# Attention heads each in their own half of the TensorE rows, paired maxima, and a causal mask set on the exponentials

## The reference

```
c_kv   = x @ W_dkv.T
q_lat  = einsum('bhtd,hdl->bhtl', q, k_eff)
attn   = einsum('bhtl,bsl->bhts', q_lat, c_kv) / sqrt(hs)      # hs = 16
attn   = where(causal_mask, -inf, attn);  attn = softmax(attn)
y      = attn times values, head by head
x      = x + layernorm(attention(layernorm(x)))
x      = x + layernorm(experts(layernorm(x)))
```

## Time and profile before

| what | value |
|---|---|
| median of 3 runs | 1568.74 us (1567.91 to 1570.16) |
| profiled execution, first to last instruction (its span; the profile gives no other time of its own) | 1560.5 us |
| median less this span | 8.2 us |
| PE busy | 1174.1 us, 75% |
| PE weight loads busy | 873.2 us, 56% |
| DVE busy | 925.3 us, 59% |
| ACT busy | 657.4 us, 42% |
| POOL busy | 340.4 us, 22% |
| mean granted TensorE clock | 0.861 |

### The profile page before, as it was taken

The page is one execution under the profiler, slowest core; times in us unless marked ns, Lnnn a source line. Parts: engine busy times, 40 slices in busy tenths (PEclk is TensorE's granted clock), DMA queues, the critical chain, the costliest instruction groups (busy, mean ns, idle before and its releaser), DMA issues. The chain is left out here.

```text
span 1560.5 us, 26871 instructions
## 1 busy us (share of the span) xinstructions
PE 1174.1 (75%) x8433; PEld 873.2 (56%) x8434; DVE 925.3 (59%) x2241; ACT 657.4 (42%) x1097; POOL 340.4 (22%) x316
## 2 busy tenths in 40 slices
PE   6844499999999999999933506977978979899000
PEld 3423255555555555555423406977978978899000
DVE  6514466666776666767178526576575665755245
ACT  3420055545554555555735413432433424344322
POOL 4104000000000000000036764034033030300785
PEclk9975699999999999999965557999989989899555
DMA  5973222222222222220011234122121221111324
GB/s 156 292 191 113 79 73 77 79 83 72 80 83 83 70 83 81 82 72 14 2 56 54 94 121 149 47 89 85 53 87 38 93 81 57 30 47 40 93 80 157
DMA packets 82934, 133.23 MB, mean 85 GB/s; under 512 B 26549, under 2 KB 53445, under 8 KB 82789
## 3 DMA queue, kind: packets, MB, share of 16 engines
q1 hardware_dynamic: 67304, 80.83, 17.1%
q0 software_dynamic: 15552, 51.42, 10.2%
HBM read 75.82 MB, written 55.87 MB: 84 GB/s over the span
## 5 line engine op out<-in xcount | busy, mean ns | idle before, releaser
L699 DVE TENSOR_REDUCE att_pm<-att_ps_m 128x1 f32<-128x512 f32 (+3 forms) x640 | 353.2, 592 | 168.9 <-PE att_ps_m L559 98.5
L673 ACT ACTIVATE att_pt<-att_ps_s 128x1024 f32<-128x1024 f32 (+3 forms) x384 | 304.8, 811 | 272.1 <-PE att_ps_s L600 192.2
L1354 ACT ACTIVATE moe_hf<-moe_ps_h,moe_b 128x256 f32<-128x256 f32 x288 | 136.9, 475 | 296.3 <-PE moe_ps_h L1305 238.6
L556 PE MATMUL att_ps_m<-att_k,att_q 128*128 128x512 f32 (+3 forms) x576 | 213.6, 420 | 10.7 <-DMA att_v<-vs 9.2
L1380 DVE TENSOR_TENSOR moe_hTl<-moe_hf,moe_hTh 128x256 fp32r<-128x256 f32 x288 | 165.4, 574 | 9.8
L596 PE MATMUL att_ps_s<-att_q,att_k 128*128 128x512 f32 (+3 forms) x576 | 164.1, 369 | 1.6 <-ACT att_pt L673 1.6
L556 PEld LDWEIGHTS att_ps_m<-att_k,att_q 128*128 128x128 f32 x576 | 112.8, 199 | 85.0 <-issue 76.7
L1378 DVE CAST moe_hTh<-moe_hf 128x256 fp32r<-128x256 f32 x288 | 118.9, 413 | 32.7 <-ACT moe_hf L1354 32.7
L613 PE MATMUL att_ps_o<-att_pt,att_v 128*17 128x512 f32 (+3 forms) x1152 | 118.8, 491 | 0.0
L559 PE MATMUL att_ps_m<-keep_mask_ts,keep_identb 128*128 128x128 bf16 x512 | 118.5, 237 | 0.0
L596 PEld LDWEIGHTS att_ps_s<-att_q,att_k 128*128 128x128 f32 x576 | 96.2, 192 | 33.2 <-ACT att_pt L673 25.6
(11 more groups left out here) (203 smaller groups left out, 2530.3 us busy)
## 6 DMA issues: line engine op xcount, KB each, us to landing
weights_raw<-in_w POOLq DMA_DIRECT2D x14, 1024.0 KB, 7.3
ys<-att_zeros POOLq DMA_DIRECT2D x10, 1024.0 KB, 9.5
moe_rows<-xs SPq DMA_DIRECT2D x38, 256.0 KB, 2.7
ys<-moe_o SPq DMA_DIRECT2D x36, 256.0 KB, 2.2
att_q<-qs SPq DMA_DIRECT2D x48, 128.0 KB
att_k<-ks SPq DMA_DIRECT2D x48, 128.0 KB
vs<-proj_v SPq DMA_DIRECT2D x32, 136.0 KB, 7.6
proj_x<-in_x POOLq DMA_DIRECT2D x8, 512.0 KB, 6.3
```

The costliest lines, as they stand in the source:

```text
L556: ins = pe.matmul(out[:, n * keys:(n + 1) * keys], qg[slot][:, h // 2, i * P:(i + 1) * P], kg[slot][:, h, k0:k0 + keys], start=True, stop= ...
L673: act.activation(pt[:, blk % 3, 2 * p:2 * p + 2, off:CH], ps_s[k % 2][:, :, off:CH], ACT.Exp, scale=HS ** -0.5).then_inc(ex_done, 1)
L699: return dve.tensor_reduce(pm[:, g % 2, i, piece, h:h + 1], src, AX.X, ALU.max)
L1354: act.activation(hf[:, f % NHB], ps_h[f % NHB][:], ACT.Relu, bias=b1[r][:, f:f + 1]).then_inc(hf_done, 1)
```

## The change

- Keys are stored like queries: `k` has two places of 128 rows instead of four, head `h` in rows `64*(h%2)` on. Each matmul of queries and keys reads only the 50 rows of its head (`rows = slice(64*e, 64*e + KM)`), and the matmuls of the heads `e = 0` and `e = 1` are issued one behind the other into different banks. The zeros and their memsets are gone, with the waits for them.
- Units are made two at a time. A pair waits for both of its banks, and signals both at its end. There are 38 units a group instead of 44: the 128-key rest of row block 4 shares a bank with row block 0, and the 256-key rests of row block 5 are two heads to a bank. The maxima are kept in another order (`pm`), and one reduction can write two places.
- The mask of a unit's diagonal block is two accumulating matmuls of 64 columns and 64 rows, `pick` times `future`, for each head.
- The exponent pass has no mask matmul. GpSimd sets the exponentials above the diagonal to zero in place (`affine_select` on 128 x 4 x 128 values) for the 8 diagonal blocks of the 12, after the second exponential of the block; the values of these blocks wait for it (`masked`).
- The two turns of the maxima move from after steps 15 and 17 to after step 18. All jobs of a step come ahead of its value block; before, only the first did.
- The clears of `ys` (16 of 640 rows) and the loads of `keep_xf` move from GpSimd's queue to SyncE's.

```
     slots["q"].append(s.sb(f"q{g}", [P, 2, T], F32R))
-    slots["k"].append(s.sb(f"k{g}", [P, GH, T], F32R))
+    slots["k"].append(s.sb(f"k{g}", [P, 2, T], F32R))
...
+    for e in range(2):
+        add((e, e + 2), ((0, 0, P, 0), (4, CH, P, 8)))
+    for e in range(2):
+        add((e, e + 2), ((1, 0, 2 * P, 1),))
+    for i in range(2, TB):
+        for h in range(GH):
+            add((h,), ((i, 0, min(CH, (i + 1) * P), i),))
+        if i == 5:
+            for e in range(2):
+                add((e, e + 2), ((i, CH, 2 * P, 4 + i),))
+        if i > 5:
+            for h in range(GH):
+                add((h,), ((i, CH, (i - 3) * P, 4 + i),))
...
-        out[step].append(job)
+        out[step] += [(kind, more, m), (kind, more, m + 1)]
...
-    out[15].insert(0, ("turn", 1, 0))
-    out[17].insert(0, ("turn", 1, 1))
+    out[18] += [("turn", 1, 0), ("turn", 1, 1)]
...
+                        sp.dma_start(d["ys"][bass.ds(b * (NG * blank_rows) + g * blank_rows, blank_rows), :]
+                        if g == 1:
+                            sp.dma_start(keep["xf"][:, bass.ds(b * TB, TB)],
...
-                for g in range(1, NSL):
-                    pool.memset(qg[g][:].bitcast(F32), 0.0).then_inc(slots["init"][g], 1)
-                    pool.memset(kg[g][:].bitcast(F32), 0.0).then_inc(slots["init"][g], 1)
...
+                            past = pt[:, blk % 3, :, off:off + P]
+                            pool.wait_ge(ex_done, at(b, g, NS, 2 * blk + 2 + 2))
+                            pool.affine_select(past, past, [[0, GH], [1, P]], ALU.is_ge, 0.0, base=0,
+                                               channel_multiplier=-1).then_inc(masked, 1)
...
+                    for e in range(2):
+                        free(b, n + e)
...
+                            for e in range(2):
+                                h = UNITS[m + e][0][pair]
+                                rows = slice(64 * e, 64 * e + KM)
+                                last[e] = pe.matmul(ps_m[(n + e) % NBK][:, at_col:end], qg[slot][rows, h // 2, i * P:(i + 1) * P],
+                                                    kg[slot][rows, h // 2, k0:k0 + keys], start=True, stop=not diag)
+                            if diag:
+                                for z in range(2):
+                                    for e in range(2):
+                                        last[e] = pe.matmul(ps_m[(n + e) % NBK][:, col:col + P // 2], pick[rows, z], future[rows, z],
+                                                            start=False, stop=z == 1)
...
-                    if diag:
-                        for e in range(2):
-                            ins = pe.matmul(out[:, e, off:off + P], identb[:], keep["mask_st"][:], start=False, stop=True)
...
-                    pe.wait_ge(ex_done, at(b, g, NS, 2 * blk + 2 + 2))
+                    if blk in DIAG:
+                        pe.wait_ge(masked, at(b, g, len(DIAG), DIAG.index(blk) + 1))
```

More of the change, by code:

```diff
@@ L382, in max_units, with add @@
     out = []
[L383 to L388, removed]
+    def add(heads, pieces):
+        out.append((heads, pieces))
+    for e in range(2):
[11 more added lines that the diff above has]
+                add((h,), ((i, CH, (i - 3) * P, 4 + i),))
     return out
@@ L547, in _, with free, units @@
                 pe.matmul(ps_o[:], onesb[:, 0:P], onesb[:], start=True, stop=True)
-                def unit(b, g, m, out):
-                    i, piece, heads, k0, keys = UNITS[m]
+                def free(b, n):
+                    if not (isinstance(b, int) and n < NBK):
+                        pe.wait_ge(bank_read[n % NBK], turns(b, n))
+                def units(b, g, m, n):
+                    pieces = UNITS[m][1]
                     slot = g % NSL
@@ L575, in turn_out, with jobs @@
                     return ins
-                def job(b, g, what, n):
-                    kind, more, m = what
-                    bank = n % NBK
-                    if not (isinstance(b, int) and n < NBK):
-                        pe.wait_ge(bank_read[bank], turns(b, n))
-                    do = {"unit": unit, "turn": max_turn, "out": turn_out}[kind]
-                    do(b, g + more, m, ps_m[bank]).then_inc(bank_made[bank], 1)
+                def jobs(b, g, todo):
+                    for (kind, more, m), n in todo:
+                        if kind == "unit":
+                            if m % 2 == 0:
+                                units(b, g + more, m, n)
+                            continue
+                        free(b, n)
+                        do = {"turn": max_turn, "out": turn_out}[kind]
+                        do(b, g + more, m, ps_m[n % NBK]).then_inc(bank_made[n % NBK], 1)
                 def scores(b, g, k):
@@ L615, in values @@
                     ins.then_inc(pv_done, 1)
-                for n, what in enumerate(first):
-                    job(0, 0, what, n)
+                jobs(0, 0, [(what, n) for n, what in enumerate(first)])
                 def body(b):
@@ L623, in body @@
                             scores(b, g, k)
[L624 to L626 removed]
+                            jobs(b, g, steps[k])
                             if k % 2 == 1 and k >= 3:
                                 values(b, g, k // 2 - 1)
[L629 to L630 removed]
                         values(b, g, NB - 1)
@@ L635, in _ @@
                 body(B - 1)
-                job(B - 1, NG, ("out", 0, 0), numbered(B - 1)[1])
+                jobs(B - 1, NG, [(("out", 0, 0), numbered(B - 1)[1])])
             @block.scalar
```

139 lines of the change are left out of this document (76 added, 63 removed).

## The result

The changed kernel takes **1636.9 us** (median of 4 runs, 1623.4 to 1640.8) against 1568.4 us for the kernel before on the same chip: a ratio of 1.042, 95% interval 1.038 to 1.047. It is 4.2% slower, outside the range of 1415 to 1545 us. The page of the changed kernel's profile gives the first hint: the span, TensorE's busy time, the clock granted to it in 40 slices, and the new work of GpSimd.

What follows compares the result with a forecast made beforehand. TensorE alone was taken to set each group's pace. Gains of 61.6 (14 groups), 3.5 (last two) and 5.7 us (start), 70.8 in all, took 1560.5 to 1489.7, with 8.2 between span and median 1498 us; range 1415 to 1545.

Steps and rivals of the forecast that it cites:

- the sum 24.1 + 6.4 + 1.9: One full attention group: TensorE's own work, bank waits and select waits, 32.4 us, taken as 32.5 instead of 36.9.
- The clock falls: Rival, chance 0.07: waits let TensorE's clock drop to 0.50 half the time; a group takes 43 us, the kernel 1650.
- the last two: Last two attention groups: expected to gain 3.5 us together.
- Scores, units, overlap: TensorE in a group: both row halves run at once, so scores take 4.6 us and units with masks 7.1.
- Length of a group at the full clock: One full attention group, forecast at 32.5 us against 36.9 before, gained 14 times: 61.6 us.
- Bank wait: TensorE waits for reductions to free two banks: 9 of 19 pairs lose about 0.7 us each, 6.4 a group.
- Select: GpSimd's mask on the exponentials: 0.7 us for 512 values; value blocks wait about 1.9 us a group.
- the rule on data-dependent branches: In the slow-GpSimd rival (0.08): 12 cycles an element, an estimated 5.1 us per 512-value select, 41 us a group.
- Start: Attention's start: without the memsets SyncE's loads and the first scores come 5.7 us earlier, first score near 191.7.
- the 0.95 that I named as the sign: Sign of being wrong: TensorE's clock in a group falling under 0.95.
- Changes of form: TensorE switching between forms of matmul: taken as now, 2.1 us a group.
- a rule by which they would add 11 us: Changing tiling mode drains TensorE: four turns drain twice each, 0.8 us a group, some 11 us in all.

Runs made afterwards that it cites:

- e3: The changed kernel with units made one at a time, each waiting for its own bank alone, halves alternating: 1635.3 us, ratio to before 1.039.
- e9: The changed kernel with all units, masks and scores reading the lower half of the rows, so nothing overlaps: 1949.9 us, ratio to before 1.240.
- e11: e9 plus 512-column filler pairs ahead of each score block, both in the same lower half: 2228.9 us, ratio to before 1.422.
- e8: The changed kernel plus useless 128-column matmul pairs, one in each half of the rows, ahead of each score pair: 1606.4 us, ratio to before 1.023.
- e6: The changed kernel plus useless 256-column matmul pairs, one in each half of the rows, ahead of each score pair: 1550.3 us, ratio to before 0.987.
- e1: The changed kernel plus useless 512-column matmul pairs, one in each half of the rows, ahead of each score pair: 1562.4 us, ratio to before 0.995.
- e7: The kernel before with GpSimd's select replacing exponent-pass masks and score pairs reading half the rows each, units at full height: 1599.2 us, ratio 1.016.

## Why the prediction was wrong

The step that failed is the forecast's silent premise that a group runs at the full clock as before: the sum 24.1 + 6.4 + 1.9 has nothing for the clock, and the rival that had it, "The clock falls", got 0.07. The clock was 0.72, and it cost some 8 to 9 us a group, 117 to 127 us in all. The span came out 147.4 us over the forecast's 1489.7. It lies, by the same stages: the 14 groups 131.8 (598.4 against 528.2 - 61.6), the last two 11.9 (they were to gain 3.5 and lost 8.4), the stages behind 5.3, the start -1.6.

- **Scores, units, overlap: right.** Pairs start 3 ns apart in the median, where I asked for within 10. The Trainium skill, TensorE: Matmul & The Clock Gate, Part 3, has small matmuls in different row groups start about 4 ns apart; the trace agrees.
- **Length of a group at the full clock: nearly right.** 33.8 us was measured for a group of e3, and 33.0 to 33.9 follows for the changed kernel, against 32.5 forecast: 0.5 to 1.4 us too low, 7 to 19 us of the 131.8.
- **Bank wait: right in size.** TensorE's matmuls stand idle for the reductions for 5.2 us in the third group, against 6.4. Making the units singly does not win it back: in e3 this idle time is 1.2 us, but most units then no longer start together, and the group is as long as before.
- **Select: right in length, its waits smaller.** 0.634 us each against 0.7 taken. In the third group TensorE's matmuls stand idle for it for 0.6 us and its weight loads for 1.5, against 1.9 in the sum. The 5.1 us that I worked out for the rule on data-dependent branches is eight times the measured length, so the rule does not fit this operation.
- **Start: nearly right.** The first score stands at 190.8 where I had 191.7, and the first exponential gained 7.3 us where I had 5.7.
- **The clock: wrong.** Over 14 groups the changed kernel is at 0.72, far under the 0.95 that I named as the sign. A mean group takes 598.4 / 14 = 42.74 us; less 33.9 and 0.56 for the jumps, or less 33.0 and 0.67 (the same two lines), 8.3 to 9.0 us are the clock's, 117 to 127 us in all. The rival's price, 43 us a group and 1650 us, was within 1% of the result, in part by luck: it put the clock's share at 11 us and the rest at 32.5, and the two errors nearly cancel. Its chance was too small. I argued against it that values and scores fill TensorE far more than in the first units. That looked at how much of the time the engine is occupied. The runs show something else: with TensorE 97% and 98% busy over the 14 groups, in one half (e9, e11), the clock is 0.52 and 0.50, and with fewer matmuls running at once in both halves it is 0.72; each added stretch with both halves at work raises it (e8, e6, e1). The kernel before covers all rows with its matmuls, half of them with zeros, and stands at 0.99.
- **The reason I gave for the rival was wrong as well.** I feared the waits. e3 takes most of them away and nothing follows; e9 all but removes them and the clock drops further. In the earlier trace rows the lower clock did come at full height, after 3.4 us in which TensorE had been busy for 2.82, so there is another way to lose it than this one.
- **Changes of form** I took as they were, and named a rule by which they would add 11 us. In e7 they are dear (the Trainium skill, TensorEngine Tiling (Array Packing), Key Properties, says that a change of mode drains the engine; the trace agrees, at 0.2 us behind a 512-column pair). In the changed kernel most units and scores have one form, so what is left of them lies in the 0.5 to 1.4 us.

What stays open: the profile grants a clock, it does not say what it is granted for. That the rows in use count is shown by the runs; by what measure they count is not. It could be the length for which both halves work at once, or the work of all matmuls, rows times columns, in a microsecond; no run was made to tell them apart. The first does not order all the kernels: e3 has far fewer unit pairs that run at once than the changed kernel and a clock no lower. The second, counted over the 14 groups with the value blocks in, does put all 14 kernels in the order of their clocks, but a lower clock also lowers the work in a microsecond, so the order alone proves little. The 0.76 of e3 against 0.72 is no difference to explain: one of the changed kernel's executions has e3's clock, 0.764, at nearly the same time (1623.4 us against 1625.0).

## What to carry to other kernels

Matmuls in halves of the rows do run at once, but work so compressed can lose more by a lower clock than it saves: before counting on it, ask of each stretch how many of the rows its matmuls use, not only how busy the engine will be. If the clock falls, keep to one form of matmul and try a little filler that covers all rows in that form (here 256 columns a block, 0.6 us a group against a gain of 87 us in all). Time the parts of a change alone: here one part was worth 21 us and was hidden by the other.

## What the hardware showed that I had not expected

- TensorE can be busy for 98% of 1141.7 us and be granted 0.50 (1.2 GHz) throughout, if scores, units, masks and filler all use the same half of the rows and only the value blocks and turns use all of them (e11). The Trainium skill, TensorE: Matmul & The Clock Gate, Part 1, has the clock follow how busy the engine has been and says that activity releases it. No amount of streaming in one half did here; the measurement decides.
- Useless work made a kernel 87 us faster (e6 against the changed kernel).
- GpSimd's select over 128 x 512 values took 0.634 us. That is near the cast of the earlier trace rows (1.95 us for 2048 values, so 0.49 for 512), and far from the two-operand row (1.16).
- A pair of half-height matmuls between full-height ones took 0.43 us, where the pair alone needs 0.23 (e7).
